# Norm and k projection of the next sequence moved into the softmax and slot stages; seams and slot stages rewritten

## The reference

```python
x = x + attn_a(_layernorm(x))   # q, k, v projections, 4-tap causal convolutions, SiLU, delta rule in
                                # chunks of 32, causal filters of 7 and 25 taps, a router, two RMS norms, Wo
x = x + ffn(_layernorm(x))      # the slot layer, below
x = x + attn_b(_layernorm(x))   # causal softmax attention, 16 heads of 16
x = x + ffn(_layernorm(x))      # the slot layer again, same weights
```

```python
h = gelu(ctx @ w1.T + b1)
route_logits = (h @ w2.T + b2) / (abs(tau) + 0.1)
alpha = softmax over the 8 largest of 64 route_logits, 0 elsewhere
gi = einsum('bts,btd->bsd', alpha, x) / (alpha.sum(1) + 1e-8)
r = sigmoid(xr + hr); z = sigmoid(xz + hz)      # x* from gi @ wih.T + bih, h* from the slots, constant
n = tanh(xn + r * hn); h_new = (1 - z) * n + z * hs
out = alpha @ (h_new @ wv.T + bv) @ wo.T + bo
```

## Time and profile before

| | |
|---|---|
| median of 3 runs | 8387.36 us (8381.74 to 8402.19) |
| profiled execution: its time | 8374.86 us |
| its span, first to last instruction | 8373.1 us, mean granted TensorE clock 0.950 |
| ScalarE busy | 3367.4 us (40%) |
| DMA queues, hardware kind | 260.09 MB, 15.3% of 16 engines |

### The profile page before, as it was taken

How to read it: one execution, slowest core, us unless ns; L and a number is a source line. 1 busy time by engine, 2 the same in 40 slices (tenths; PEclk the granted TensorE clock), 3 DMA queues, 4 the chain that set the end, 5 groups by cost and what they waited for, 6 DMA issues and landing times. The chain is left out here.

```text
span 8373.1 us, 122632 instructions
## 1 busy us (share of the span) xinstructions
PE 7421.8 (89%) x47710; PEld 4285.2 (51%) x47710; DVE 4866.4 (58%) x9426; ACT 3367.4 (40%) x6875; POOL 1783.2 (21%) x2689
## 2 busy tenths in 40 slices
PE   6899988989888998888988899888888888998898
PEld 4546455464554645546455464554645546455464
DVE  5465664656646566564665656656466564665646
ACT  2252533525335253352533525335253352534425
POOL 2112121121211222112121122211222112221221
PEclk9999999999999999998999999999999999999999
DMA  2021111101112011120111202111021110211102
GB/s 72 16 38 24 32 46 23 42 13 32 46 24 44 10 32 46 24 44 10 32 46 24 44 10 37 41 29 42 8 37 41 32 46 1 37 41 31 46 2 41
DMA packets 337786, 268.71 MB, mean 32 GB/s; under 512 B 213521, under 2 KB 276369, under 8 KB 337097
## 3 DMA queue, kind: packets, MB, share of 16 engines
q1 hardware_dynamic: 337148, 260.09, 15.3%
HBM read 48.71 MB, written 42.02 MB: 11 GB/s over the span
## 5 line engine op out<-in xcount | busy, mean ns | idle before, releaser
L1791 ACT ACTIVATE sa_pt<-ps 128x512 f32<-128x512 f32 (+3 forms) x3072 | 1271.9, 492 | 728.8 <-PE ps L1779 723.3
L1716 DVE TENSOR_REDUCE sa_nm<-ps 128x2 f32<-128x1024 f32 (+4 forms) x1280 | 1389.1, 1114 | 281.5 <-PE ps L1697 138.1
L1779 PE MATMUL ps<-sa_qs,sa_ks 99*128 99x512 bf16 (+3 forms) x3072 | 795.8, 333 | 76.3 <-ACT sa_pt L1791 58.3
L1798 POOL TENSOR_SCALAR_AFFINE_SELECT sa_pt<-sa_pt 128x512 f32<-128x512 f32 x512 | 325.2, 635 | 1703.1 <-ACT sa_pt L1791 1700.6
L1697 PE MATMUL ps<-sa_ks,sa_qs 96*128 96x512 bf16 (+3 forms) x2560 | 631.0, 321 | 57.5 <-DVE sa_nm L1716 36.9
L1811 PE MATMUL ps<-sa_pt,sa_va 128*17 128x512 f32 (+3 forms) x6144 | 644.9, 492 | 8.2 <-POOL sa_pt L1798 8.2
L312 PE MATMUL ps<-identb 128*128 128x512 bf16 x2608 | 626.9, 388 | 10.4 <-ACT dr_z L1061 10.4
L1779 PEld LDWEIGHTS ps<-sa_qs,sa_ks 99*128 99x128 bf16 x3072 | 257.8, 97 | 651.9 <-ACT sa_pt L1791 473.6
L609 PE MATMUL ps<-rep,stack 128*32 128x512 f32 x4608 | 529.2, 611 | 41.9 <-DMA rep<-paths 41.9
L280 POOL TENSOR_TENSOR rstd<-vare,mhalf 128x2 f32<-128x2 f32 x260 | 181.0, 696 | 1248.5 <-DVE vare L272 1248.5
L857 POOL TENSOR_TENSOR A<-paths 128x256 f32<-128x256 f32 x384 | 271.9, 740 | 799.7 <-DVE paths L1027 799.7
(11 more groups left out here) (353 smaller groups left out, 14070.1 us busy)
## 6 DMA issues: line engine op xcount, KB each, us to landing
sa_qs<-sa_parts SPq DMA_DIRECT2D x288, 128.0 KB, 5.0
sa_ks<-sa_parts SPq DMA_DIRECT2D x288, 128.0 KB, 5.8
x<-in_x SPq DMA_DIRECT2D x17, 1024.0 KB, 5.6
rep<-paths SPq DMA_DIRECT2D x128, 128.0 KB, 2.4
bounce<-paths SPq DMA_DIRECT2D x32, 512.0 KB, 2.8
out_y<-x SPq DMA_DIRECT2D x32, 512.0 KB, 3.0
rep<-paths SPq DMA_DIRECT2D x128, 127.9 KB, 2.4
rep<-paths SPq DMA_DIRECT2D x128, 127.8 KB, 3.2
```

The source lines that it names most:

```text
L1716: nc.vector.tensor_reduce(nm[:, g % 2, op.c, op.t, op.j:op.j + op.heads], cols, AX.X, ALU.max, negate=True).then_inc(s.slot_free, 1)
L1779: last = nc.tensor.matmul(bank[:, off:], ks[0:QROWS, g % NBUF, j, kt * P:(kt + 1) * P], qs[0:QROWS, g % NBUF, j, n * BANK + off:(n + 1) * ...
L1791: nc.scalar.activation(pt[:, gs % 2, j, off:BANK], ring_bank(ring_use(gs, j))[:, off:], ACT.Exp, scale=RATIO).then_inc(s.ring_out, 1)
L1798: nc.gpsimd.affine_select(block, block, [[0, GH], [1, P]], ALU.is_ge, 0.0, base=0, channel_multiplier=-1).then_inc(s.masked, 1)
```

## The change

- `first_norm` and the last slot stage: besides the norm and the turning, the k projection of the next sequence (`project_key_pe`, `keep_key_act`) and the first tap of its convolution (`key_tap_act`) are done there. The convolution stage starts with the v projection, and DVE with the three other taps of k.
- The load of `x0` moves from the last slot stage to the first one; the norm of the next sequence (`next_statistics`, `next_deviations`, `next_normalise`) goes into the head of the softmax stage and is written to the space of `qT`. Its turning and two k products lie in front of the wait for `alpha` of the last slot stage, the other two behind the gates.
- Seams: the first four tiles are turned before the block ends, then 12 (10 in the softmax stage) `keep_warm`, then the last four; the copies to `xnT` are in the old block too.
- Slot stages: `b2` and `w2` are scaled by `invtau` in `setup`, `b2` is added by a product with the identity on TensorE, DVE reads the logits in PSUM; the gather has the tokens' features as the stationary side and 64 moving columns (16 products in place of 8) and needs no turning of `gi`; the division by `wsum` moves behind the gates; the gates' arithmetic is rearranged, with parts beside the tanh.
- `pre`, `k_tm` and `qT` have fixed places; the softmax stage's `pt` lies in `pre` and its `otm` in `k_tm`.

The core of the diff:

```diff
-                keep_warm(nc, k, ps[:, 0, :], 8)
+                turn_pe(nc, k, ps, s, pe, 0, 0)
+                keep_warm(nc, k, ps[:, 2, :], 12)
+                turn_pe(nc, k, ps, s, pe, 0, 1)
...
 # slot_ffn, TensorE
-                turn_normed_pe(nc, k, ps, s)
...
+                nc.tensor.matmul(ps[:, 2, :], k.ident[:], k.b2[:].unsqueeze(1).to_broadcast([P, T, SLOTS]),
+                                 start=True, stop=False, skip_group_check=True)
...
-                keep_warm(nc, k, ps[:, 7, :], 30)
+                if store is None:
+                    keep_warm(nc, k, ps[:, 7, :], 30)
+                else:
+                    for n in range(NB):
+                        turn_next_pe(nc, k, ps, s, n)
+                    keep_warm(nc, k, ps[:, 3, :], 3)
+                    for u in range(HALVES):
+                        project_key_pe(nc, k, ps, s, pe, u)
+                    keep_warm(nc, k, ps[:, 3, :], 5)
+                    pe.wait_ge(s.next_kept, HALVES * NB)
                 pe.wait_ge(s.alpha, 1)
                 for t in range(T):
-                    last = nc.tensor.matmul(ps[0:SLOTS, 3, 0:D + 1], alpha[:, t, :], k.xn[:, t, :],
-                                            start=(t == 0), stop=(t == T - 1))
+                    for a in range(HALVES):
+                        last = nc.tensor.matmul(ps[:, 6, a * SLOTS:(a + 1) * SLOTS], k.xn[:, t, a * P:(a + 1) * P],
+                                                alpha[:, t, :], start=(t == 0 and a == 0), stop=(t == T - 1),
+                                                skip_group_check=True)
...
+                    for u in range(HALVES, len(KEYS)):
+                        project_key_pe(nc, k, ps, s, pe, u)
 # slot_ffn, DVE
-                settle(nc.vector.tensor_tensor(lg[:], ps[:, 2, :].rearrange("p (t n) -> p t n", t=T),
-                                               k.b2[:].unsqueeze(1).to_broadcast([P, T, SLOTS]), ALU.add))
-                settle(nc.vector.tensor_scalar(lg[:], lg[:], k.invtau[:, 0:1], None, ALU.mult))
...
-                if store is not None:
-                    dve.wait_ge(io.loaded, 16)
-                    for u in range(T // 2):
-                        norm_statistics(nc, k, s, settle, k.x0, u)
...
-                settle(nc.vector.tensor_scalar(rz[:], rz[:], 0.5, 0.5, ALU.mult, ALU.add))
-                settle(nc.vector.tensor_tensor(mem[:], rz[:, 0:D], k.hn[:], ALU.mult))
-                settle(nc.vector.tensor_tensor(mem[:], mem[:], k.bihn[:], ALU.add))
+                settle(nc.vector.scalar_tensor_tensor(mem[:], rz[:, 0:D], 1.0, k.hn[:], ALU.add, ALU.mult))
+                nc.vector.tensor_tensor(new[:], gates_n[:], mem[:], ALU.add).then_inc(s.n_in, 1)
+                settle(nc.vector.tensor_scalar(fresh[:], rz[:, D:2 * D], -0.5, 0.5, ALU.mult, ALU.add))
+                settle(nc.vector.scalar_tensor_tensor(carried[:], rz[:, D:2 * D], 1.0, k.hs[:], ALU.add, ALU.mult))
...
 # softmax_attention, POOL, ACT, DVE
+                next_deviations(nc, k, s, pool)
                 split_max_pool(pool, settle, 0)
...
+                next_normalise(nc, k, s, act)
                 act.wait_ge(s.third, 2 * HALVES * NB)
...
+                    if u % 2:
+                        dve.wait_ge(io.loaded, 16)
+                        next_statistics(nc, k, s, settle, u // 2)
                 max_dve(dve, 0, max_ops_before(0))
...
 # project_and_convolve, TensorE and ACT
-            for i, w in enumerate((k.wk, k.wv)):
-                for a in range(HALVES):
-                    project(i, w, a)
+            for a in range(HALVES):
+                project(1, k.wv, a)
...
-            for a in range(HALVES):
-                evacuate(0, a)
-                first_tap(0, a)
```

More of the change, by code:

```diff
@@ L330, in turn_normed_dve, with turn_pe @@
-def turn_normed_dve(nc, k, ps, s, dve):
-    for n in range(NB):
-        dve.wait_ge(s.xn_turned, HALVES * n + 2)
-        nc.vector.tensor_copy(k.xnT[:, 1, n * BANK:(n + 1) * BANK], ps[:, 4 + HALVES * n + 1, :]).then_inc(s.xn1, 1)
-def first_norm(nc, k, ps, s, io):
+def turn_pe(nc, k, ps, s, pe, first, n):
+    pe.wait_ge(s.xn_normed, (n + 1) * (BANK // P))
+    for a in range(HALVES):
+        for i in range(BANK // P):
+            last = nc.tensor.transpose(ps[:, first + HALVES * n + a, i * P:(i + 1) * P],
+                                       k.xn[:, n * (BANK // P) + i, a * P:(a + 1) * P], k.ident[:])
+        last.then_inc(s.xn_turned, 1)
@@ new lines, with turn_next_pe, turn_next_act @@
+KEYS = [(a, n) for n in range(NB) for a in range(HALVES)]
+KEY_BANKS = (0, 1, 4, 5)
+NEXT = ((4, 5), (6, 7))
+def turn_next_pe(nc, k, ps, s, n):
+    for a in range(HALVES):
+        for i in range(BANK // P):
+            last = nc.tensor.transpose(ps[:, NEXT[n][a], i * P:(i + 1) * P],
+                                       next_tokens(k)[:, n * (BANK // P) + i, a * P:(a + 1) * P], k.ident[:])
+        last.then_inc(s.next_turned, 1)
+def turn_next_act(nc, k, ps, s, act, n):
+    for a in range(HALVES):
+        act.wait_ge(s.next_turned, HALVES * n + a + 1)
+        nc.scalar.activation(k.xnT[:, a, n * BANK:(n + 1) * BANK], ps[:, NEXT[n][a], :], ACT.Copy).then_inc(s.next_kept, 1)
@@ new lines, in project_key_pe, with keep_key_act @@
+def project_key_pe(nc, k, ps, s, pe, u):
+    a, n = KEYS[u]
+    pe.wait_ge(s.next_kept, HALVES * (n + 1))
+    for c in range(HALVES):
+        last = nc.tensor.matmul(ps[:, KEY_BANKS[u], :], k.wk[:, c, a * P:(a + 1) * P], k.xnT[:, c, n * BANK:(n + 1) * BANK],
+                                start=(c == 0), stop=(c == HALVES - 1))
+    last.then_inc(s.key_ps, 1)
+def keep_key_act(nc, k, ps, s, act, u):
+    a, n = KEYS[u]
+    act.wait_ge(s.key_ps, u + 1)
+    nc.scalar.activation(k.pre[:, 0, a, 3 + n * BANK:3 + (n + 1) * BANK], ps[:, KEY_BANKS[u], :], ACT.Copy).then_inc(s.key_kept, 1)
@@ L597, in _ @@
             keep_warm(nc, k, ps[:, ROWS[0], :], 4)
[L598 removed]
+            pe.wait_ge(s.padded, 1)
             pe.wait_ge(s.a, T)
@@ L1440, in _ @@
                                      ACT.Exp).then_inc(s.exp, 1)
+                if store is not None:
+                    turn_next_act(nc, k, ps, s, act, 1)
+                    for u in range(HALVES):
+                        keep_key_act(nc, k, ps, s, act, u)
                 for n in range(NB):
@@ L1519, in _ @@
                     add_with_statistics(nc, k, s, dve, settle, lambda u: ps[:, u, :])
+                    for n in range(NB):
+                        turned_dve(nc, k, ps, s, dve, 4, n)
                 else:
@@ L2011, in _ @@
                     norm_statistics(nc, k, s, settle, k.x1, u)
+                for n in range(NB):
+                    turned_dve(nc, k, ps, s, dve, RING_BANK, n)
             @block.sync
@@ L2069 @@
     "mi": "part mixed square kept summed scale_in scale wide spread ot out",
-    "ff": "h_ps h logits shifted exp alpha gathered at_ps alphat gi git_ps git gates rz_in rz n_in n mem memt_ps memt "
-          "values_ps values out x_out next_normed next_turned next_kept",
+    "ff": "h_ps h logits shifted exp alpha gathered alpha_sum weighed at_ps alphat git gates rz_in rz n_in n mem memt_ps memt "
+          "values_ps values out x_out next_turned next_kept padded key_ps key_kept",
     "sa": "const ones first second third rest qk_ps v_ps v_out slot_ready slot_free merged split m_turned m_rows0 m_rows1 scores ring_out "
-          "sums o_out osb_turned pool masked stacked_late out turned ot1",
+          "sums o_out osb_turned pool masked stacked_late out turned ot1 next_var next_rstd next_normed",
 }
```

255 lines of the change are left out of this document (144 added, 111 removed).

## The result

The changed kernel takes 8323.9 us (median of 4 runs, 8321.1 to 8338.4) against 8391.5 us (8381.7 to 8402.2) for the kernel before, run beside it: ratio 0.9917, with a 95% interval from 0.9892 to 0.9942. It is faster by 0.8%, or 67.6 us, where 154 were forecast. The median is inside the range and 91 us above the predicted time: the direction was right, the size was not.

A forecast was written before the change was run, and what follows sets the result against it. TensorE, busy 89% of the span, was taken as the bound in the convolution and softmax stages. Per sequence 6.9 + 4.3 + 1.6 + 2.6 - 5.2 = 10.2 us, times 16 less 9 is 154: 8233 us, range 8165 to 8345.

The forecast's parts named there:

- convolution stage: Head of the convolution stage: 16 k projection records leave TensorE, which stays the bound; 6.9 us saved per sequence.
- head of the softmax stage: Before the first scores: tiles 4.1, statistics 0.7 and slower clock 0.4 add 5.2 us per sequence.
- seam of the mix: End of the mix: clock holds with the last eight transposes behind the last tile; 1.4 us saved, b2 product included.
- seam of the first slot stage: End of the first slot stage: 1.5 us saved, from 3.3 if the clock holds down to -1.8.
- seam of the softmax stage: End of the softmax stage: clock holds in idle time below 2 us; 1.4 us saved, b2 product included.
- inside the first slot stage: First slot stage: alpha 0.95 us earlier and gates to mem 0.65 shorter; 1.6 us saved.
- inside the last slot stage: Last slot stage: 0.7 us to alpha, 1.0 at the gather, 0.85 from gates to mem; 2.6 us saved.
- rival (c): Convolution stage: ACT or DVE becomes the bound, 3 us saved in place of 6.9; 8295 us, chance 0.11.
- rival (a): Slot stages: reads in PSUM are dear, so all of the 1.25 us comes back; 8263 us, chance 0.12.
- (b): Seams give nothing because the clock falls in the new gaps too; 8329 us, chance 0.15.
- (d): Softmax head: the norm hides there, costing 0 in place of 5.2 us; 8150 us, chance 0.08.
- (e): Softmax head exposed in full, 17.8 us in place of 5.2; 8434 us, chance 0.09.

The follow-up runs named there:

- e4: Changed kernel with 14 keep_warm products ahead of the first turning at the first slot stage's end and 10 in place of 12 behind it; 8276.7 us.
- e1: Changed kernel with ACT's eight normalised tiles of the next sequence issued ahead of the four v copies in place of behind them; 8244.5 us.
- e2: Changed kernel with the fourth pair's statistics behind the softmax head's maxima and ACT's last two tiles behind the first exponentials; 8258.8 us.
- e6: Changed kernel with the k projection's 16 records issued once more behind the v projection, result unused; 8450.6 us.
- e3: Changed kernel with six tiles ahead of the v copies, two behind the first exponentials, fourth pair's statistics behind the head's maxima; 8191.0 us.
- e8: Kernel before, old seams kept, with longer keep_warm filler: 20 for 8 at mix and softmax ends, 28 for 8 at first slot stage's end; 8368.9 us.

## Why the prediction was wrong in size

The terms per sequence, forecast and measured, with their miss (positive: worse than forecast):

```
                                          forecast  measured   miss
convolution stage                            -6.9     -6.6     +0.3
head of the softmax stage                    +5.2     +8.8     +3.6
seam of the mix                              -1.4     -1.4      0.0
seam of the first slot stage                 -1.5     +0.7     +2.2
seam of the softmax stage                    -1.4     +0.2     +1.6
inside the first slot stage                  -1.6     -2.3     -0.7
inside the last slot stage                   -2.6     -3.3     -0.7
sum                                         -10.2     -4.0     +6.2
```

(The sum holds -0.1 for the stretches between the convolution stage and the mix.) The one-time cost, forecast at 9 us, is 9.24, which the first sequence doesn't save, + 0.61 by which its v projection starts later, 9.85 in all. 16 times 3.98 less 9.85 is 53.8 us, the distance of the two profiled executions.

**Seams: the step that failed most**, -4.3 forecast and -0.5 measured. Two things in it were wrong, both in the price of the clock. At the end of the first slot stage I had written that the 12 `keep_warm` would last 5.1 us if the clock fell in the gap of 3.6 us, and then took 1.5, a value near the other side. It fell in every sequence (12 lasted 4.3 us), and e4 shows that this cost 1.94 us of the 2.2 missed. At the end of the softmax stage I had priced the slow clock of before at two seams of three, by the median of the transposes, and put the slow w1 products (1.2 us) on the same two thirds. Two thirds is right for all seams together, but not for each: in the trace of before transposes are slow in 14 of 16 sequences at the mix, in 11 at the first slot stage and in 6 here, and the w1 products here in 3 of 16. A transpose can be slow while the products behind it are not, so the two had to be counted by themselves, seam by seam. By these rows the slow clock cost 0.6 us here (2.32 - 1.94 and 0.2 for w1), where I took 2.1. At the mix it cost 1.7: more transposes were slow than I took and fewer w1 products (5 of 16), so that the 0.0 of that row is partly luck. The mechanism, transposes at 273 ns, came true; there was less to win than I counted.

**Head of the softmax stage: +5.2 forecast, +8.8 measured.** The first scores came 7.7 us later, where 4 to 5 were forecast. The tiles came as written: 4.1 forecast, 3.99 by e1. The statistics were put at 0.7 and cost 2.2 us before the first maximum (e2), of which 0.96 is the stretched operation. The slow clock was put at 0.4 and cost 2.3 (e2): I had looked for it in the wait before the scores only, and it came already 20 us earlier, in a wait of 1.92 us that the statistics themselves made. That wait lies in front of v products which the earlier trace rows don't show and which the forecast never priced. And the long stretch behind the first scores lost another 1.07, the slow clock that I had looked for: e1, where it is gone, gives 1.93 us back. The kernel before has no low clock behind its first scores in 8 of 16 sequences, and takes 129.4 us in these.

**Convolution stage**, right for the reason given. L530's counterpart came 17.8 us behind the first product, later than the 16 to 17 given as a sign: the last sequence, from which the 23.4 of before was read, is with 23.42 among the shortest of 16, whose mean is 24.32. The slow start fell on v, and rival (c) is refuted by e6.

**Slot stages**, right in mechanism and too cautious by 1.4 us in all. From logits to MAX8 1.25 us went, and the short operations that now read PSUM gave back 0.07 and 0.16 us of it where I took 0.3: rival (a) is refuted. The section named in the prediction ("VectorE: DVE Perf Modes", "⚠️ The TRN2 errata" of the Trainium skill) would have it, by the estimate made there, at 1.2 us; the trace doesn't agree. Eight MAX8 took 1.11 us from SBUF and 1.15 from PSUM. The gather was 4.9 us, not 5.3, in both stages, so that the first one gained 0.44 where I took nothing.

**The rivals.** (b), "the seams give nothing", names what happened at two of three seams, and its time of 8329 is nearest to the measured 8324; but that is luck: its sum got there without the softmax head's 3.6 us, and with gains of the slot stages that were too small. (d) and (e) are refuted for the changed kernel, and e3 shows that (d) was nearly to be had by a change of place alone: from the first q product to the last scores 162.6 us, before 162.4. The bound that would have called the forecast wrong, over 8 us in the softmax head, was passed.

**Still open**: in some sequences the seam of the mix takes 20.5 us in place of 17.4: in none of the changed kernel and of e6, in one to four of 16 in the other runs, in e8 four. The 3 us lie before and in the projection of the mix and not at the turning, and they are slow clock: in the fourth sequence of e3 it is 0.50 from 1832.2 to 1838.8, and the spreading runs in that time. Why it falls there in these sequences alone was not tried. In e8 the gain of the seams was not divided further.

## What to carry to other kernels

An instruction put into an engine's list is free only where the engine waits and nothing later in its list is awaited: look for the wait, and then for who waits behind it. Where an edit leaves TensorE idle (1.3 to 4.5 us here), price the products behind the gap at half clock, as the likely case and not as the bad one, and fill the gap with products that end with it, not after it. After such an edit look again at the seams that were not touched, since they can lose the clock when everything before them moves by a few us.

## What the hardware showed that I had not expected

- A DVE operation on 2 columns, 163 ns in the median of its 68 runs, lasted 1129 ns when it started at 8113.85 under two POOL operations that ran from 8112.67 to 8114.95, and ended with them. The same form at another line took 0.64 us under a POOL operation of 0.63. The statistics operations in front of it were not stretched. In the changed kernel this happens in all 16 sequences; in e2, where the operation runs later, none of the 68 lasts over 0.17 us. This fits what the Trainium skill says in "SBUF — State Buffer", section "🔬 SBUF: two separate sides": a DVE operation in a mode with two ports and a GpSimd operation exclude each other from a shared pair of ports, and the one that comes second blocks for the whole instruction. That this operation ran in such a mode no row shows, so that part of the cause is argued; that it has to do with its place, and the 0.96 us, are measured.
- The granted clock of a seam can change by an edit elsewhere. The w1 products of the last slot stage ran at full clock in 16 of 16 sequences of the changed kernel and in none of e1, with the same code at that seam. The idle time in front of the last turning was 1.12 to 1.17 us in the one and 1.29 to 1.89 us in the other.
- Filler lasts longer when it starts at half clock: 12 products of 512 columns took 4.30 us, where 10 take 2.32 at full clock.
- A wait can cost more than its length: TensorE's 4.54 us in front of the first scores were followed by 8.3 us at half clock, which cost another 1.9 us.
